# Projection weights split a stage early, weights of the last two stages loaded in the sixth stage, and a last stage in three float32r passes

## The reference

```python
x = _layernorm(x + _L0_attn_ref(...))   # Mamba-2 scan
x = _layernorm(x + _L0_ffn_ref(...))    # int8 weights: silu(x Wg sg) * (x Wu su), then Wd sd
x = _layernorm(x + _L1_attn_ref(...))   # 16 heads of 128
x = _layernorm(x + _L1_ffn_ref(...))    # mixture of 32 experts
x = _layernorm(x + _L2_attn_ref(...))   # Mamba scan
x = _layernorm(x + _L2_ffn_ref(...))    # ternary weights
x = _layernorm(x + _L3_attn_ref(...))   # 16 heads of 16, with its own feed-forward of 1024
x = _layernorm(x + _L3_ffn_ref(...))    # feed-forward of 688 with LoRA experts
# _L1_attn_ref: q, k, v = x @ w_qkv (256 x 6144), then w_o (2048 x 256)
# _L3_ffn_ref, E = 8 experts, rank R = 8, two of them per token with weights w:
gate = x @ W_gate + (x @ sA_gate) @ sB_gate / R + ((x A_gate) B_gate / R * w).sum(experts)
up   = ...the same with W_up...
hidden = silu(gate) * up                # 688 wide
out = hidden @ W_down + ...the same two LoRA terms with sA_down, A_down...
```

## Time and profile before

| | |
|---|---|
| runs (3) | 2817.5, 2817.87, 2819.13 us, median 2817.87 |
| profiled execution, its own time | 2824.52 us |
| its span, first to last instruction | 2822.8 us |
| PE / ACT / DVE / POOL busy | 82% / 50% / 61% / 28% of the span |
| mean granted TensorE clock | 0.902 of full speed |
| `l0_ffn` | 322 to 456 us |
| `l1_attn` | 456 to about 1010 us |
| `l2_ffn` | 1996 to 2144 us |
| `l3_attn` | 2144 to 2555 us |
| `l3_ffn`, then the output | 2555 to 2823 us |

### The profile page before, as it was taken

The page is one execution under the profiler, slowest core; times in us unless marked ns, Lnnn a source line. Parts: engine busy times, 40 slices in busy tenths (PEclk is TensorE's granted clock), DMA queues, the critical chain, the costliest instruction groups (busy, mean ns, idle before and its releaser), DMA issues. The chain is left out here.

```text
span 2822.8 us, 47695 instructions
## 1 busy us (share of the span) xinstructions
...
## 2 busy tenths in 40 slices
...
GB/s 123 0 0 0 14 0 119 1 2 2 3 2 3 2 247 135 116 117 102 115 57 46 46 46 46 57 35 1 23 0 42 1 1 0 0 0 43 0 0 30
DMA packets 77709, 111.40 MB, mean 39 GB/s; under 512 B 15162, under 2 KB 64050, under 8 KB 76484
## 3 DMA queue, kind: packets, MB, share of 16 engines
...
...
## 5 line engine op out<-in xcount | busy, mean ns | idle before, releaser
L1756 POOL TENSOR_TENSOR l2a_hb<-l2a_hb,l2a_Cb 128x1024 f32<-128x1024 f32 x128 | 303.2, 2380 | 112.8 <-DVE l2a_hb L2212 111.8
L2212 DVE TENSOR_TENSOR_SCAN l2a_hb<-l2a_dA,l2a_dB 128x1024 f32<-128x1024 f32 x128 | 288.4, 2274 | 63.0 <-PE l2a_dB L1837 30.1
L2066 ACT ACTIVATE l2a_dA<-l2a_delta,l2a_An 128x255 f32<-128x255 f32 x512 | 214.4, 497 | 37.2 <-DVE l2a_delta L2152 20.9
L1837 PE MATMUL l2a_dB<-l2a_diag,l2a_dxT 64*128 64x128 f32 x2048 | 190.9, 308 | 31.1 <-DVE l2a_hb L2212 18.3
L1837 PEld LDWEIGHTS l2a_dB<-l2a_diag,l2a_dxT 64*128 64x128 f32 x2048 | 141.5, 196 | 95.4 <-PE l2a_dB L1837 37.5
L793 PE MATMUL l1a_QK<-l1a_xh,l1a_wqkv_h 128*128 128x256 f32 x512 | 146.7, 286 | 13.7 <-DVE l1a_wo L1022 10.4
L793 PE MATMUL l1a_QK<-l1a_xh,l1a_wqkv 128*128 128x256 f32 x512 | 145.6, 284 | 0.0
L793 PE MATMUL l1a_QK<-l1a_xl,l1a_wqkv_h 128*128 128x256 f32 x512 | 145.4, 284 | 0.0
L1857 PE MATMUL l2a_YS<-ident,l2a_hb 128*128 128x128 f32 x1024 | 143.3, 287 | 1.0 <-POOL l2a_hb L1756 1.0
L1001 ACT ACTIVATE l1a_ex<-l1a_S,l1a_nm 128x256 f32<-128x256 f32 x256 | 119.2, 471 | 36.9 <-DVE l1a_nm L1053 36.9
L1857 PEld LDWEIGHTS l2a_YS<-ident,l2a_hb 128*128 128x128 f32 x1024 | 117.4, 146 | 12.4 <-issue 1.7
...
## 6 DMA issues: line engine op xcount, KB each, us to landing
...
```

The lines of the kernel that those rows point to most:

```text
L1756: nc.gpsimd.tensor_tensor(h[:, :, :], h[:, :, :], Cb[p][:, s0:s0 + UN, :], ALU.mult).then_inc(hc_ready, 1)
L1837: last = nc.tensor.matmul(out[:, m:m + 2, j * P + a:j * P + a + HP], dxT[q][a:a + HP, j, c * P:(c + 1) * P], diag[q][a:a + HP, j, s0 + m:s ...
L2066: last = nc.scalar.activation(dA[(i * NU + u) % DAS][:, n, 1:SEQ], delta[q][:, c, 1:SEQ], ACT.Exp, scale=An[:, c, s0 + n:s0 + n + 1])
L2212: nc.vector.tensor_tensor_scan(flat(hb[u % RING]), flat(dA[(i * NU + u) % DAS]), dB[u % 2][:, :], 0.0, ALU.mult, ALU.add).then_inc(scanned, 1)
```

## The change

Four things are changed.

1. `w_qkv` is loaded and split in `l0_ffn`, items 2 to 7, four pieces of 128x512 per item (24 in all), into tiles that live until `l1_attn` ends. ACT copies a piece at its steps 4 to 7, DVE subtracts one at its steps 5 to 8.
2. `l1_attn` splits only the four pieces of `w_o`, in the first item, at steps 3 to 6 of ACT and DVE, as the last thing in the step. PE waits for them in front of the output of heads 0, 4, 8 and 12.
3. The 23 loads of `l3_attn` and the 21 of `l3_ffn` are issued in `l2_ffn`, behind that stage's own three, into tiles of their own.
4. `l3_ffn` is written as a pipeline over items: gate, up and down in three float32r passes, the end of an item (`turn_haw`, `finish_down`, residual, normalization) inside the next one. The router product, the last LoRA term and the turns stay in float32. Its weights are split at the head of the stage. ACT copies the turned item twice (`xh`, then `xT`).

```diff
@@ l0_ffn @@
+            sp.wait_ge(w_cast, 3)
+            for m in range(PIECES):
+                if m >= SLOTS:
+                    sp.wait_ge(early.low_ready, m - SLOTS + 1)
+                sp.dma_start(raw[m % SLOTS][:, :].bitcast(F32), early.src[:, kc, c:c + 512]).then_inc(qkv_loaded[m % SLOTS], 16)
@@ l0_ffn, scalar, behind the copy of ah @@
+                    if 4 <= step < 4 + SLOTS and split:
+                        act.wait_ge(qkv_loaded[step - 4], (i - 1) * 16)
+                        nc.scalar.copy(high[:, i * 4 - 8 + step - 4, :], raw[step - 4][:, :].bitcast(F32)).then_inc(early.high_ready, 1)
@@ l0_ffn, vector, end of a step @@
+                    if 5 <= step < 5 + SLOTS and split:
+                        n = i * 4 - 8 + step - 5
+                        dve.wait_ge(early.high_ready, n + 1)
+                        nc.vector.tensor_tensor(low[:, n, :], raw[step - 5][:, :].bitcast(F32), high[:, n, :].bitcast(F32),
+                                                ALU.subtract).then_inc(early.low_ready, 1)
@@ l1_attn @@
-                        if first and h % GROUP == 0:
-                            pe.wait_ge(w_low, (h // GROUP + 1) * 4)
+                        if first and h % GROUP == 0:
+                            pe.wait_ge(w_low, h // GROUP + 1)
-            for m in range(len(PIECES)):
-                act.wait_ge(w_loaded[m % SLOTS], 16 * (m // SLOTS + 1))
-                nc.scalar.copy(high, came).then_inc(w_high, 1)
+                    if first and 3 <= step < 3 + PIECES:
+                        act.wait_ge(w_loaded[(step - 3) % SLOTS], 16 * ((step - 3) // SLOTS + 1))
+                        nc.scalar.copy(high, came).then_inc(w_high, 1)
@@ l2_ffn, sync @@
+            sh.late.load_l3_attn(sp)
+            sh.late.load_l3_ffn(sp)
@@ l3_attn @@
-            pe.wait_ge(w_loaded, 16 * 5)
+            pe.wait_ge(l3a_loaded, late.L3A)
@@ l3_ffn, tensor @@
+            def item(i, p, first=False):
+                pe.wait_ge(xl_ready, i + 1)
+                for f, rows in CH:
+                    if not first or f >= 3:
+                        pe.wait_ge(gu_used, i * FC + f - 2)
+                    if f == 0:
+                        pe.wait_ge(xaw_low, i + 1)
+                    for half, wh, wl, bh, bl in ((0, wgh, wgl, bgh, bgl), (1, wuh, wul, buh, bul)):
+                        parts = [(wh[:, kc, cols], wl[:, kc, cols], xh[p][:, kc, :], xl[p][:, kc, :]) for kc in range(KC)]
+                        parts += [(bh[:, cols], bl[:, cols], xawh[:, p, half, :], xawl[:, p, half, :])]
+                        last = product(nc.tensor, GU[n % 3][0:rows, half * SEQ:(half + 1) * SEQ], parts)
+                    if f == 0:
+                        if not first:
+                            turn_haw(i - 1)
+                        turn(ph, pe, i + 1)
+                    if f == 1 and not first:
+                        finish_down(i - 1)
+                    if f == 2:
+                        router_and_a(pe, i + 1, 1 - p)
+                for j in range(NT):
+                    for f, rows in CH:
+                        if j == 0:
+                            pe.wait_ge(hid_low, i * FC + f + 1)
+                        if j == 0 and f == FC - 1:
+                            turn_xaw(pe, i + 1)
+                        last = product(nc.tensor, YB[j][:, 0:D + LR],
+                                       [(hh[0:rows, f, tile], hl[0:rows, f, tile], wdh[0:rows, f, :], wdl[0:rows, f, :])],
+                                       first=(f == 0), last=(f == FC - 1))
@@ l3_ffn, vector, one item @@
+                        nc.vector.tensor_tensor(hid[0:rows, n % 3, :], GU[n % 3][0:rows, SEQ:2 * SEQ], gs[0:rows, n % 3, :], ALU.mult
+                                                ).then_inc(gu_used, 1)
+                    if step >= 1:
+                        dve.wait_ge(hid_high, i * FC + f + 1)
+                        nc.vector.tensor_tensor(hl[0:rows, f, :], hid[0:rows, n % 3, :], hh[0:rows, f, :].bitcast(F32), ALU.subtract
+                                                ).then_inc(hid_low, 1)
+                    if step == 0:
+                        low_x(dve, i + 1, 1 - p)
+                    if step == 2 and not first:
+                        residual(i - 1)
+                    if step == 3:
+                        route(dve, i + 1, 1 - p)
+                    if step == 5 and not first:
+                        normalize(ph, dve, i - 1)
+                low_xaw(dve, i + 1, 1 - p)
```

More of the change, by code:

```diff
@@ L647, in l0_ffn @@
         GU = [ph.ps(f"GU{n}") for n in range(NB)]
+        early = sh.early
+        SLOTS = 4
+        low, high = (t[:, :, :].rearrange("p k (m n) -> p (k m) n", n=512) for t in (early.wqkv, early.wqkv_h))
+        PIECES = high.shape[1]
+        assert PIECES == SLOTS * (ITEMS - 2)
+        qkv_loaded = ph.semaphores(" ".join(f"qkv_loaded{n}" for n in range(SLOTS)))
         block = ctx.enter_context(nc.Block())
@@ L716, in _, with item @@
         def _(act):
-            def item(i, p, first=False):
+            def item(i, p, first=False, split=False):
                 for step in range(FC + 1):
@@ L740, in _ @@
                 for p in range(2):
-                    item(it * 2 + p, p)
+                    item(it * 2 + p, p, split=True)
         @block.vector
@@ L1081, in item @@
                         normalize(ph, dve, i - 1)
+                    if first and 3 <= step < 3 + PIECES:
+                        dve.wait_ge(w_high, step - 2)
+                        _, came, high, low = piece(step - 3)
+                        nc.vector.tensor_tensor(low, came, high.bitcast(F32), ALU.subtract).then_inc(w_low, 1)
                     if step == TURN + 2:
@@ new lines, in item @@
+            def item(i, p, first=False):
+                for step in range(FC + 1):
+                    if step < FC:
+                        f, rows = CH[step]
+                        n = p * FC + f
+                        act.wait_ge(gu_ready, i * FC + f + 1)
+                        if not first or f >= 3:
+                            act.wait_ge(gu_used, i * FC + f - 2)
+                        nc.scalar.activation(gs[0:rows, n % 3, :], GU[n % 3][0:rows, 0:SEQ], ACT.Silu).then_inc(silu_ready, 1)
+                    if step == 0:
+                        if not first:
+                            keep_hawT(i - 1)
+                        keep_x(act, i + 1, 1 - p)
+                    if step == 3:
+                        scores(act, i + 1)
+                    if step >= 1:
+                        f, rows = CH[step - 1]
+                        n = p * FC + f
+                        act.wait_ge(gu_used, i * FC + f + 1)
+                        if f == 0:
+                            act.wait_ge(down_ready, i * NT)
+                        nc.scalar.copy(hh[0:rows, f, :], hid[0:rows, n % 3, :]).then_inc(hid_high, 1)
+                high_xaw(act, i + 1, 1 - p)
@@ new lines, in _ @@
+            keep_x(act, 0, 0)
+            act.wait_ge(l3f_loaded, late.L3F)
+            scores(act, 0)
+            for raw, high, _ in SPLITS[:4]:
+                nc.scalar.copy(high, raw).then_inc(w_high, 1)
+            high_xaw(act, 0, 0)
+            for raw, high, _ in SPLITS[4:]:
+                nc.scalar.copy(high, raw).then_inc(w_high, 1)
+            item(0, 0, first=True)
+            item(1, 1)
+            with act.Fori(1, ITEMS // 2) as it:
+                for p in range(2):
+                    item(it * 2 + p, p)
@@ new lines, in _ @@
+            for n, (raw, high, low) in enumerate(SPLITS):
+                if n == 4:
+                    low_xaw(dve, 0, 0)
+                dve.wait_ge(w_high, n + 1)
+                nc.vector.tensor_tensor(low, raw, high.bitcast(F32), ALU.subtract).then_inc(w_low, 1)
+            item(0, 0, first=True)
+            item(1, 1)
+            with dve.Fori(1, ITEMS // 2) as it:
+                for p in range(2):
+                    item(it * 2 + p, p)
+            residual(ITEMS - 1)
+            normalize(ph, dve, ITEMS - 1)
@@ L3288, in program @@
         for phase in PHASES if phases is None else phases:
+            if phase is l0_ffn:
+                early = ExitStack()
+                sh.early = EarlyWeights(nc, early, sh, w)
+            if phase is l2_ffn:
+                sh.late = LateWeights(nc, ctx, w)
             phase(nc, sh, w)
+            if phase is l1_attn:
+                early.close()
             nc.all_engine_barrier(sems_to_clear=PHASE_SEMS)
```

365 lines of the change are left out of this document (198 added, 167 removed).

## The result

| | before | after |
|---|---|---|
| median of 4 runs | 2818.5 us | 2734.45 us |
| profiled execution's span | 2822.8 us | 2731.3 us |
| PE / ACT / DVE busy | 82% / 50% / 61% | 84% / 53% / 64% |
| mean granted TensorE clock | 0.902 | 0.911 |

The ratio is 0.9698, with a 95% interval of 0.9681 to 0.9715: 84 us less, where 72 were forecast (2746, range 2725 to 2772). Of all runs of all kernels here one, in experiment 9, was slow (7272.7 us at a granted clock of 0.32); every time given is of the others.

What follows compares the result with a forecast made beforehand. PE idles during weight splits at the third stage's start and waits for DMAs later; products limit the last stage. 25.5 - 8.6 + 15.1 + 45.1 - 5 = 72 us off 2824.5 gives 2752.5, 2746 on the runs' scale; range 2725 to 2772.

Steps and rivals of the forecast that it cites:

- Part 1: Start of l1_attn: without the w_qkv split, first S 31.5 us earlier; four w_o pieces cost 6; net gain 25.5.
- Part 2: In l0_ffn, three subtractions ahead of the last al lengthen each item by 1.43 us: 8.6 us lost over six items.
- Part 3: Loads issued in l2_ffn: queries of l3_attn start 15.1 us earlier, first gate product of l3_ffn 11.2 us earlier.
- Part 4: In l3_ffn, three passes bring items from 28.28 to 23.9 us; with the head of the stage, gain 45.1 us.
- The head: Start of l3_ffn: with early loads, less the weight splits, the first gate product comes 11.2 us sooner.
- The clock: Items of l0_ffn and l3_ffn: new waits lower TensorE's clock, a quarter of 14 x 1.3 us, 5 lost (0 to 18).
- The clock rival: TensorE's clock drops in nearly every changed item, costing 13 us more: 2759; chance 0.13.
- the ACT and DVE bound: Last stage: route, table loads and copies line up, items of 26 to 28 us, 2763 to 2775; chance 0.11.
- the slow last stage: Last stage: PE at the lower clock for most items, 43.4 us each against 28.3; all eight give 2896; chance 0.03.
- The splits: Rival: steps of l0_ffn and the first l1_attn item absorb DVE's split work, 8.6 and 4 to 6 back, 2731; chance 0.09.

Runs made afterwards that it cites:

- experiment 9: The changed kernel with the four w_qkv subtractions of an l0_ffn item moved behind its last low part on DVE: 2718.8 us, ratio 0.9666.
- w_back: The changed kernel with padding around the two w_qkv tiles so they begin at a multiple of 128 bytes, as before: 2740.8 us, ratio 0.9745.
- experiment 11: The kernel of experiment 9 with w_o pieces spread over the first item, and l3_ffn down products reordered chunk by chunk: 2699.5 us, ratio 0.9594.

## Why the prediction was right, and where it was off

**Part 1, sized right, and one effect missing.** The shift of the first item less four pieces was forecast at 25.5. With the effect of the placement taken out, as `w_back` does, the first normalization came 26.1 us earlier (125.9 to 99.8). The first `S` came 30.9 us earlier (36.26 to 5.40 behind the low part of x) of 31.5. A `w_o` piece cost 1.6 us a step (forecast 1.77). What failed is an assumption under the whole sum, which has no term for it: that items which the diff doesn't touch take the same time. Products with `w_qkv` became shorter because its tiles lie differently. By the stage table the change gained 85.1 us where 72.1 were forecast, and 12.3 of these 13.0 are in `l1_attn`; `w_back` gives 11.8 of them back (518.8 against 507.0). That this landed inside the range is luck: the range was made of other terms.

**Part 2, right.** Forecast 1.43 us an item and 8.6 in all, measured 1.24 (15.32 against 14.08) and 6.9, and experiment 9 shows the mechanism: moved into DVE's wait, the same subtractions cost nothing.

**Part 3, right.** 15.1 forecast, 14.9 measured, and the waits for DMAs are gone. The queries start 2.39 us behind the turn's start instead of 17.35, which is 15.0.

**Part 4, right.** The head gave 10.2 us (first gate product 18.6 behind the last addition at L154 of `l3_attn`, 28.8 before) of 11.2. An undisturbed item took 24.07 of 23.9, with waits of 1.5 (forecast 2) and 22.6 of work (forecast 21.8). The waits stand behind `route`, as forecast. The extra work I read as late products (last section); with fewer of them experiment 11 does the same products in 21.5. Late starts aside, a product of 256 columns took about 0.118 us and one of 328 columns 0.150, against 0.119 and 0.152 in the sum.

**The clock, where the term came out by luck.** Inside the items of `l3_ffn` it fell once: for 10.2 us from 2612.1 on TensorE was busy all the time at 0.5, the lower of the two levels. The item from 2609.76 to 2638.34, which has waits of 1.13 and 0.46 at its start like every other, took 28.6 us, 4.5 more than its neighbours. In `l0_ffn`, with waits of 1.6 to 1.7, the clock stayed at 1.00 from 335 to 448 us. The term was 5, but for a quarter of 14 drops at 1.3 us each: there was one, and it cost three times as much. The Trainium skill (TensorE: Matmul & The Clock Gate, A second HAM failure mode: psum-queue depth-cycling) tells of a kernel in which short idles between groups of products made the clock swing; here waits of this kind cost one drop in 14 items.

The other traces say more. In each of the nine that have this last stage with its waits for `hl` exactly one item holds a drop, of 10.2 us in six and 3.4 us in three, and takes 4.5 or 1.6 us more; which item it is differs. In the two that have the products of experiment 11, where these waits are gone, no drop comes before the tail of the last item. In the three with the last stage of the kernel before, which waits 1.00 and 0.72 us in each item of 28.28, there is none either. So the drop goes with these waits, but a wait of such a length alone doesn't bring it.

```profile
2612.10:2622.30 10.20, 10.20 (x38) 9.14 (x38) 1.06 (x3) 0.58 (x1) 0.00 (x0) 0.50 0.00 0
...
2615.00:2639.00 24.00, 22.94 (x151) 21.67 (x150) 9.55 (x42) 8.25 (x18) 1.45 (x3) 0.85 0.00 0
...
2639.00:2663.00 24.00, 22.49 (x167) 20.96 (x166) 11.22 (x47) 8.80 (x20) 1.45 (x3) 1.00 0.00 0
```

**The rivals.** The clock rival, the ACT and DVE bound and the slow last stage didn't come. The splits don't hide: experiment 9 got back 7 us that those in `l0_ffn` cost, and the four steps with `w_o` stand in the trace as 1.6 us longer each, which spreading them only moved. The last stage is neither bound by ACT nor DVE: with another order of products TensorE works without a break at 21.5 us an item. The low end of that rival, 2763, was added up wrong: six items at 2.1 make 2759.
